# Key and value expansions from stacked high and low latents, a third PSUM bank for the score maxima, and ScalarE as the issuer of the stages' transfers

## The reference

```
x = x + 0.5 * ffn(layernorm(x))
x = x + attn(layernorm(x))
x = x + 0.5 * ffn(layernorm(x))

attn: kv_c = rmsnorm(x @ W_kv) * g_kv                      # rank 64
      q_c  = x @ W_q                                       # rank 128
      q = [q_c @ W_qdec , rope(q_c @ W_qrope)]             # 16 heads, 16 + 32
      k = [kv_c @ W_kdec, rope(x @ W_krope)]
      v = kv_c @ W_vdec                                    # 16 heads, 16
      softmax(causal(q k^T / sqrt(48))) v @ W_o
ffn:  x W^T + b + sum over the top 2 of 8 experts of gate_e * B_e (A_e x)   # rank 16
```

## Time and profile before

| what | value |
|---|---|
| median of three runs | 2007.97 us (2002.25 to 2008.69) |
| the profiled execution's own time | 2005.28 us |
| its span, first to last instruction | 2002.8 us |
| PE busy | 1901.2 us (95%) |
| DVE busy | 1439.5 us (72%) |
| ACT busy | 1024.3 us (51%) |
| mean granted clock of TensorE | 0.98 |

### The profile page before, as it was taken

The page is one execution under the profiler, slowest core; times in us unless marked ns, Lnnn a source line. Parts: engine busy times, 40 slices in busy tenths (PEclk is TensorE's granted clock), DMA queues, the critical chain, the costliest instruction groups (busy, mean ns, idle before and its releaser), DMA issues.

```text
span 2002.8 us, 32215 instructions
## 1 busy us (share of the span) xinstructions
PE 1901.2 (95%) x10832; PEld 1325.5 (66%) x10832; DVE 1439.5 (72%) x4555; ACT 1024.3 (51%) x2125; POOL 849.4 (42%) x912
## 2 busy tenths in 40 slices
PE   6789999999999999999999999999999999999995
PEld 5446766666677666766677667666767667677554
DVE  5767777777776877778777777788777687677632
ACT  3436554555454554545555545555556455454450
POOL 3446453553433635255441644435453454422121
PEclk9979999999999999999999999999999999999997
DMA  3687666676665666676566576646677566665511
GB/s 101 191 207 173 169 153 173 163 173 152 174 157 123 175 159 162 164 168 162 152 155 162 145 196 161 167 115 171 168 166 196 129 172 160 159 155 122 116 33 45
DMA packets 169812, 307.58 MB, mean 154 GB/s; under 512 B 15088, under 2 KB 33776, under 8 KB 169648
## 3 DMA queue, kind: packets, MB, share of 16 engines
q1 hardware_dynamic: 169648, 305.53, 61.0%
HBM read 179.12 MB, written 126.35 MB: 153 GB/s over the span
## 4 chain that ended last, share of the span: by engine, by line
PE 68%; DMA 10%; DVE 8%; POOL 7%; ACT 2%; issue 2%; SPq 1%; POOLq 0%; DVEq 0%; ACTq 0%
PE st_b L755 12%; PE o_b L775 11%; PE mx_b L787 11%; PE st_b L757 10%; PE tp_b L824 4%; PE wj_b L712 4%; DMA st<-k_scratch 3%; PE tp_b L821 3%; PE wj_b L681 2%; PE wj_b L714 2%; DMA q_scratch<-lo_t 2%; PE wj_b L699 2%; DVE xn L1077 2%; PE wj_b L692 2%; DVE mx_b L977 1%
## 5 line engine op out<-in xcount | busy, mean ns | idle before, releaser
L859 ACT ACTIVATE probs<-st_b 128x512 f32<-128x512 f32 (+3 forms) x1536 | 708.3, 489 | 537.9 <-PE st_b L757 504.4
L977 DVE CUSTOM_DVE_ANT_0 mx_b<-mx_b,tri 128x256 f32<-128x256 f32 (+3 forms) x1024 | 511.0, 515 | 141.2 <-PE mx_b L787 136.9
L755 PE MATMUL st_b<-st 97*128 97x512 f32 (+2 forms) x1536 | 588.2, 387 | 10.6 <-ACT probs L859 6.8
L787 PE MATMUL mx_b<-st 96*128 96x256 f32 (+2 forms) x1536 | 565.5, 411 | 12.4 <-DVE mx_s L980 6.3
L757 PE MATMUL st_b<-st,k_st 96*128 96x512 f32 (+2 forms) x1536 | 533.4, 351 | 0.0
L1169 POOL TENSOR_SCALAR_AFFINE_SELECT probs<-probs 128x512 f32<-128x512 f32 x256 | 168.2, 660 | 607.9 <-ACT probs L859 607.5
L980 DVE TENSOR_REDUCE mx_s<-mx_b 128x1 f32<-128x512 f32 (+1 forms) x512 | 333.2, 651 | 117.0 <-PE mx_b L787 110.4
L787 PEld LDWEIGHTS mx_b<-st 96*128 96x128 f32 x1536 | 282.0, 191 | 169.6 <-issue 80.1
L755 PEld LDWEIGHTS st_b<-st 97*128 97x128 f32 x1536 | 293.1, 191 | 134.7 <-issue 61.4
L757 PEld LDWEIGHTS st_b<-st,k_st 96*128 96x128 f32 x1536 | 294.9, 192 | 33.0 <-issue 9.8
L775 PE MATMUL o_b<-probs,v_s 128*17 128x512 f32 (+3 forms) x3072 | 285.7, 490 | 2.0 <-POOL probs L1169 1.9
(11 more groups left out here) (189 smaller groups left out, 2302.7 us busy)
## 6 DMA issues: line engine op xcount, KB each, us to landing
st<-q_scratch SPq DMA_DIRECT2D x128, 384.0 KB, 5.9
st<-k_scratch SPq DMA_DIRECT2D x128, 384.0 KB, 8.7
k_st<-k_scratch SPq DMA_DIRECT2D x128, 384.0 KB, 10.4
q_scratch<-hi_t SPq DMA_DIRECT2D x32, 768.0 KB, 3.8
q_scratch<-lo_t SPq DMA_DIRECT2D x32, 768.0 KB, 5.2
k_scratch<-hi_t SPq DMA_DIRECT2D x30, 768.0 KB, 4.3
k_scratch<-lo_t SPq DMA_DIRECT2D x30, 768.0 KB, 4.6
ao_scratch<-o_f SPq DMA_DIRECT2D x256, 32.0 KB, 1.8
```

The source lines that it names most:

```text
L755: nc.tensor.matmul(dst, k1_st[u][0:SHIFT + 1, a, P * j:P * j + P], q_st[u][0:SHIFT + 1, a, q0:q0 + w], start=True, stop=False)
L787: nc.tensor.matmul(mx_b[:, m % 2, 0:w], q_st[u][0:SHIFT, a, P * i:P * i + P], k1_st[u][0:SHIFT, a, k0:k0 + w], start=True, stop=True).then ...
L859: nc.scalar.activation(probs[:, a, PLACE[s]:PLACE[s] + n], st_b[:, a % 2, HALF - n:HALF], ACT.Exp, scale=SCALE).then_inc(exp_done, 1)
L977: nc.vector.tensor_tensor_reduce(src, src, tri[:, HALF - n:HALF], 1.0, NEG, ALU.add, ALU.max, dst).then_inc(mx_done, 1)
```

## The change

1. `kvs` becomes fp32r with the rounded latent in rows 0 to 63 and the rest (`kv_lo`, a new DVE step after ACT's `kvt` evacuation) in rows 64 to 127. The weights become `kv_w`, two fp32r tiles: high over low, and low over high. Each content-key piece and each half of a value step is two fp32r matmuls that accumulate, in place of one fp32 matmul. `fold_g` builds the tiles with five DVE instructions in place of two; four memsets of DVE go away. wkv, cos and sin are loaded into parts of the spare `hl_t` tiles.
2. `wj_b` goes from two banks to one, lane 1 keeps `o_b` alone, and `mx_b` has three banks. Each step of a job now waits until the one before is emptied; a maximum waits until the third last is reduced.
3. ACT issues `x_load`, `ao_load`, `x_store` (80 DMAs), the first loads of weights (11) and the store of each unit's high half (64), with the same waits that SP had. SP keeps the low halves, the loads of q and k, the shifts and the attention's stores.
4. The five strings are new.

```diff
@@ ORDER, one line of PE's string of before and of after (of 37)
-        "XXSSPXXSSJXSSXPXSXSXJSSXJXSXFSXVXXSSJXXSSPXXSSVXXSSPXSXSPXXSSXPXSSXXFJSXSXPXXSSXVXXSSJXXSSJXXSSVXXSSPXXS"
+        "SXXXSSPSSXXXSSPXSXXSXVXSXXSXFVSXSXXSJSXSXXJSSXPSSXXXJSSXPSSXXXJFSSXXXSVSSXXXVSSXXXSSXPSSXXXSSXPSSXXVSSXX"
...
-LAT_DVE = [..., ("norm", 1, 1), ("ss",), ("kvn",)]
+LAT_DVE = [..., ("norm", 1, 1), ("ss",), ("kvn",), ("kv_lo",)]
...
+        "D": [(name, n) for n in range(NJ) if LANE[n] == 0 for name in LOADS[JOBS[n][0]]],
+        "d": [(name, n) for n in range(NJ) if LANE[n] == 1 for name in LOADS[JOBS[n][0]]],
+        "u": [("store", n, 0) for n in range(NU)],
...
     "SP": {
-        "u": [("store", n, hl) for n in range(NU) for hl in range(2)],
+        "u": [("store", n, 1) for n in range(NU)],
...
-        mx_b = bank("mx_b", 2)
+        mx_b = bank("mx_b", 3)
...
-        wj_b = bank("wj_b", 2)
-        lanes = [Lane(sb, [wj_b[:, 0, :], wj_b[:, 1, :]], ...
-                 Lane(carve, [o_b[:, 0, :], st_b[:, 1, :]], ...
+        wj_b = bank("wj_b")
+        lanes = [Lane(sb, [wj_b[:, 0, :]], ...
+                 Lane(carve, [o_b[:, 0, :]], ...
...
                 use = bank_use(n, name)
-                if name == "wo0" and use:
+                if use:
                     pe.wait_ge(own.wj_free, use)
-                elif use > 1:
-                    pe.wait_ge(own.wj_free, use - 1)
...
-                    if NM * g + m > 1:
-                        pe.wait_ge(mx_done, NM * g + m - 1)
-                    nc.tensor.matmul(mx_b[:, m % 2, 0:w], q_st[u][0:SHIFT, a, P * i:P * i + P],
+                    if NM * g + m > 2:
+                        pe.wait_ge(mx_done, NM * g + m - 2)
+                    nc.tensor.matmul(mx_b[:, (NM * g + m) % 3, 0:w], q_st[u][0:SHIFT, a, P * i:P * i + P],
...
-                        last = nc.tensor.matmul(dst, wk_s[:, eight], own.kvs[:, :, :], start=True, stop=True)
+                        for kk in range(2):
+                            last = nc.tensor.matmul(dst, kv_w[kk][:, 0, eight], own.kvs[:, :, :], start=(kk == 0),
+                                                    stop=(kk == 1))
...
-                        last = nc.tensor.matmul(tp_b[:, 0, D * k:D * k + D].rearrange("p (q n) -> p q n", q=NQ),
-                                                own.kvs[:, 2 * tt + k, :], wkv_s[:, :, HQ * DC:2 * HQ * DC],
-                                                start=True, stop=True)
+                        for kk in range(2):
+                            last = nc.tensor.matmul(tp_b[:, 0, D * k:D * k + D], own.kvs[:, 2 * tt + k, :],
+                                                    kv_w[kk][:, 1, :], start=(kk == 0), stop=(kk == 1))
...
+                elif name == "x_load":
...
+                        act.wait_ge(own.stored, 16 * done)
...
+                    nc.scalar.dma_start(own.xa[:, :, :], x_g[k] if kind == JOB_A else x1_d[k]).then_inc(own.x_in, 16)
...
+                elif name == "x_store":
...
+                    act.wait_ge(own.wj_free, bank_use(n, "y1") + 1)
...
+                elif name == "store":
+                    act.wait_ge(hic_done, n + 1)
+                    act.wait_ge(hir_done, n + 1)
+                    scratch_free(act, n)
+                    nc.scalar.dma_start(scratch_rows(n, 0), hl_t[SPARE[n]][0][:, :, :].bitcast(F32)).then_inc(
+                        hl_out[SPARE[n]][0], 16)
...
+                elif name == "kv_lo":
+                    dve.wait_ge(own.kv_hi, count(g, 1) + 1)
+                    nc.vector.tensor_tensor(own.kvs[KR:P, :, :], wj_of(g, "kvt")[0:KR, :].rearrange("p (t n) -> p t n", n=P),
+                                            own.kvs[0:KR, :, :].bitcast(F32), ALU.subtract).then_inc(own.wj_free, 1)
```

More of the change, by code:

```diff
@@ L183 @@
+        "VSSSJSSJSSSVSSSSSJSSJSSJSSVJSSSVJJJjjjjjjjjj",
         "",
@@ L283 @@
 FFN_DVE += [("route", k) for k in range(RT)] + [("gated",), ("y", 0), ("y", 1)]
-LAT_DVE = [("stats", 1, 0), ("stats", 1, 1), ("aggr", 1), ("norm", 1, 0), ("norm", 1, 1), ("ss",), ("kvn",)]
+LAT_DVE = [("stats", 1, 0), ("stats", 1, 1), ("aggr", 1), ("norm", 1, 0), ("norm", 1, 1), ("ss",), ("kvn",), ("kv_lo",)]
 WO_DVE = [("wo", 0), ("wo", 1)]
@@ L332 @@
         "a": quads(("ao", 0), ("ao", 1)),
-        "J": [(name, n) for n in range(NJ) if LANE[n] == 0 for name in SP_STEPS[JOBS[n][0]]],
-        "j": [(name, n) for n in range(NJ) if LANE[n] == 1 for name in SP_STEPS[JOBS[n][0]]],
     },
@@ L419, in build @@
         wq_raw, wkr_raw = raw[:, 0:H * DQ], raw[:, H * DQ:H * DQ + KD * H * DR].rearrange("p (k n) -> p k n", k=KD)
+        wkv_raw = hl_t[0][0][0:KR, 2, :].bitcast(F32)
+        cos_s, sin_s = [hl_t[0][1][:, 2, TB * DR * i:TB * DR * (i + 1)].bitcast(F32).rearrange("p (k c) -> p k c", c=DR)
+                        for i in range(2)]
         wide = [part[:, 0:2, :].rearrange("p a t -> p (a t)").bitcast(F32) for part in hl_t[0]]
@@ L510, in wj_of @@
         def wj_of(n, name):
-            return lanes[LANE[n]].banks[bank_use(n, name) % 2]
+            return lanes[LANE[n]].banks[0]
         def last_use(m):
@@ L529, in rope, with scratch_free, scratch_rows @@
             engine.tensor_tensor(r[:, 1, :], r[:, 1, :], r[:, 0, :], ALU.add).then_inc(roped[SPARE[n]], 1)
+        def scratch_free(engine, n):
+            m, pair, side = UNIT[n]
+            b, half = divmod(m, 2)
+            if b > 1:
+                g = NQ * (b - 2) + NQ // NP * (pair + 1) - 1
+                engine.wait_ge(qk_in[g % 2][half], 64 * (g // 2 + 1))
+                engine.wait_ge(k2_in[half], 32 * (g + 1))
+        def scratch_rows(n, hl):
+            m, pair, side = UNIT[n]
+            b, half = divmod(m, 2)
+            rows = qk_d[side][b % 2, hl, PH * DQ * pair:PH * DQ * (pair + 1), HALF * half:HALF * (half + 1)]
+            return rows.rearrange("(r x) t -> r x t", x=3)
         def landed(sp, g, half):
@@ L950, in _ @@
                         dst, src = kv[0:KR, :, :], wj[0:KR, :].rearrange("p (t n) -> p t n", n=P)
-                    nc.scalar.activation(dst, src, fn).then_inc(own.wj_free, 1)
+                    nc.scalar.activation(dst, src, fn).then_inc(own.kv_hi if what == "kvt" else own.wj_free, 1)
         @block.vector
```

358 lines of the change are left out of this document (167 added, 191 removed).

## The result

The changed kernel takes 1990.33 us (median of 6 runs, 1987.31 to 1999.08), the kernel before, run beside it, 2006.97 us. The ratio is 0.9927, with a 95% interval of 0.9905 to 0.9949, so 0.7% faster. Run again later it had 1989.27 us and 0.9929 (0.9907 to 0.9952). The forecast was 1987 us, so the sum was near. Its terms were not, and this part is about them.

What follows compares the result with a forecast made beforehand. PE, 95% busy, was taken to bound the dense middle, chains through other engines the two ends. Terms -24.7 - 12 + 4 + 8 + 3 + 3 + 0 = -18.7 us took 2005.28 to 1987 us; range 1968 to 2006.

Steps and rivals of the forecast that it cites:

- Content keys and values: PE's dense middle: fp32r pairs save 0.39 us on 32 pieces and 0.19 on 64 value matmuls, all gained: -24.7 us.
- Third bank: Maxima on PE: one more may run ahead of DVE's reductions, so most waits go: -12 us, bounds 0 and -30.
- One bank for a job's steps: Job steps on PE: each waits 0.95 us until the one before is emptied: +4 us, bounds 0 and +20.
- the end: After the last scores: last product 4.6 us earlier, 4.8 lost to lane 1's single bank: 0 us, bounds -5 and +6.
- ACT's issues: DMAs issued by ACT delay exponentials and PE: +8 us; waits for a store's landing 0 to 1 us, twice a batch.
- The layer norm wait: PE's wait for normed x, chiefly C jobs: less PE work between `wo1` and `tr0`: +3 us, bounds -10 and +20.
- The start: Up to the first score: weights on ACT end near 12.6 us, tables 2 to 3 later: +3 us, bounds -5 and +12.
- A batch: One sequence in the middle: about 233 us, not 236.

Runs made afterwards that it cites:

- fp32_kv: The changed kernel with one fp32 matmul back in place of the two fp32r ones for each content-key piece and half of the values: 2001.98 us, ratio 0.9989.
- b_stack: The kernel before with the stacked latents alone, its banks, orders and SP's issuing kept, plus one low-half DVE step per latent job: 2018.45 us, ratio 1.0086.
- lane1_two: The changed kernel with lane 1 given its second bank again, with the waits of the kernel before: 1980.80 us, ratio 0.9878.
- sp_issue: The changed kernel with all transfers issued by SP again, placed as in the changed kernel's trace: 1991.42 us, ratio 0.9939.
- after_again: The changed kernel itself, unaltered, run again later against the kernel before: 1989.27 us, ratio 0.9929.
- lane1_tail: The changed kernel with two banks for lane 1, its `wo0` and `wo1` ahead of lane 0's `y1`, and that addition behind the statistics: 1979.98 us, ratio 0.9878.

## Why the sum held and its terms did not

- *Content keys and values, -24.7.* The work is as predicted, 0.39 and 0.19 us an instruction, and fp32_kv has it back as 22.7 us in the middle. The step that failed is "both lie in PE's dense middle, so I take all of it": worth 12 us in the whole, 5 to 19 by the interval. In the order before, as placed in b_stack, it was worth nothing or less. PE at 95% busy was read as a bound; what an instruction frees goes in part into waits that move.
- *Third bank, -12.* The loads' waits fell by 57.8 - 44.0 = 13.8 us, the maxima's part by 8.5 and that of their turning by 7.6, near the term. As the price of a bank it is no number: take it away and 300 us are lost, since the new order spends it.
- *One bank for a job's steps, +4.* For lane 1 it costs 5.4 us at the end; the 10 us of lane1_two's ratio hold a start and a clock that are not shown to be the bank's. The term *the end* held this part. For lane 0 it was not tried; the rest of the jobs went from 296.2 to 301.7, which agrees.
- *ACT's issues, +8.* Nothing that can be told, 0 to 5 us; the price of an issue by itself stays open within that. ACT's wait for out_y's landing came once a batch and not twice, with 1.5 to 3.3 us and not 0 to 1, and 4.2 us of it reached PE by way of VectorE. Waits for exponentials did grow, 20.0 us in the table and 11.9 at the loads, but sp_issue has them as well (358.9 us at the first matmul of a score), so they come with the new orders and shorter pieces and not with the issues. 7.1 us of them are the one wait behind the first score, which no term had.
- *The layer norm wait, +3.* Wrong in sign and out of its bounds' lower end: -11.8 in the table. The row of 22.1 us was read as chiefly C jobs, but 10.7 of it was the first transpose of the program; nearly all of the rest went. "PE's own work between `wo1` and `tr0`" was counted rightly, but I took DVE's four steps as fixed. They were 5.4 us long because of POOL and are 1.4.
- *The start, +3.* It came as +4.4 and +2.1 (after_again). The reason given, weights issued until 12.6 us, failed: 8.22. The time goes with the lower clock up to the first score, 0.85 and 0.86 against 0.89.
- *The end, 0.* The last product 4.6 us earlier: 4.8. What the single bank costs behind it: predicted 4.8, came as 7.4. I had put `gated_tr`, `y0` and `y1` into the wait for `aoc`. But `gated_tr` waited 3.20 us for POOL and `y0` took some 5 us, at the lower clock, where I had 2.6; both held `wo0` up, and lane1_tail has that part back.
- A batch (four quads, from first score to first score, mean of the last four) went from 237.3 to 234.2 us; predicted 236 to 233.
- *The clock* is in no term. Its mean was 0.980 before and is 0.975; by the estimate above, the time would be some 11 us shorter without that.

So it was right by compensation, which is luck. The matmuls were 12.7 us too hopeful, the start and the end 1.4 and 2.6; against them stand 8 us too much for the issues and 14.8 for the norm wait, which no part of the prediction foresaw. With these errors put right the sum would be -24.8 us, and the spans differ by 15.0. The 10 us between are in no term: 7.1 are the wait behind the first score, and the rest, by size, could be the lower clock. A range built from the terms' bounds held because errors of both signs were in it.
